# Softmax denominators of a cross attention: one f32 matmul on f32 ones becomes two f16 matmuls on f16 ones, placed after the second score group of a head

## The reference, cut to what matters

```python
q = rmsnorm(q, q_norm_w)             # 8 batches, 32 heads of 128, 64 queries
k = rmsnorm(jnp.repeat(k, 4, axis=1), k_norm_w)      # 8 key heads, 1601 keys
scores = jnp.einsum('bhqd,bhkd->bhqk', q, k) * scale + attention_mask
attn = jax.nn.softmax(scores.astype(jnp.float32), axis=-1)
out = jnp.einsum('bhqk,bhkd->bhqd', attn, v)
```

## Time and profile before

| | us |
|---|---|
| median of three runs | 2546.01 (2544.3 to 2546.27) |
| the profiled execution, its own time | 2543.32 |
| its span in the trace | 2541.5 |
| of it: up to the first full step of the attention | about 230 |
| attention, steps at full pace | about 230 to 1920 |
| attention's last step and what follows it | about 1920 to 1967 |
| output projection, state-space layer, experts | the rest |

### The profile page before, as it was taken

One profiled execution on the slowest core, in us unless ns is written; L12 is line 12 of the kernel. 1 busy time (PEld: TensorE's weight loads), 2 busy tenths in 40 slices (PEclk: granted clock), 3 DMA queues, 4 the chain that ended last, 5 costly groups with the idle time before them and its releaser, 6 DMA issues. The chain is left out here.

```text
span 2541.5 us, 48195 instructions
## 1 busy us (share of the span) xinstructions
PE 2394.1 (94%) x18380; PEld 1736.5 (68%) x18380; DVE 1996.1 (79%) x2722; ACT 1252.1 (49%) x1830; POOL 1510.8 (59%) x927
## 2 busy tenths in 40 slices
PE   6879999999999999999999999999996878989995
PEld 3447878877887787788778878877885334544543
DVE  6868787888788778888878888888777548889984
ACT  4544554455455445544544554455443435555640
POOL 0116777777777777777777777777765003344432
PEclk9989999999999999999999999999998989999997
DMA  5521000100100010001010100100000921122100
GB/s 188 175 62 28 24 23 25 32 24 19 32 25 21 27 32 24 19 25 32 18 30 26 30 17 27 32 17 16 9 6 13 286 96 59 60 93 81 59 18 25
DMA packets 101092, 117.67 MB, mean 46 GB/s; under 512 B 8190, under 2 KB 70782, under 8 KB 100862
## 3 DMA queue, kind: packets, MB, share of 16 engines
q1 hardware_dynamic: 98846, 107.25, 13.3%
q0 software_dynamic: 2016, 7.34, 1.1%
HBM read 96.74 MB, written 17.83 MB: 45 GB/s over the span
## 5 line engine op out<-in xcount | busy, mean ns | idle before, releaser
L176 POOL TENSOR_TENSOR p_l<-S,p_h 128x1792 f16<-128x1792 f32 x126 | 422.5, 3354 | 285.9 <-ACT p_h L444 285.9
L550 DVE SCALAR_TENSOR_TENSOR S<-pS,rk,mask 128x256 f32<-128x256 f32 x832 | 359.9, 478 | 137.3 <-PE pS L244 130.6
L244 PE MATMUL pF<-w_l,ctx_h 128*128 128x256 f16 (+1 forms) x1664 | 453.5, 273 | 0.0
L244 PE MATMUL pF<-w_h,ctx_l 128*128 128x256 f16 (+1 forms) x1664 | 453.5, 273 | 0.0
L244 PE MATMUL pF<-w_h,ctx_h 128*128 128x256 f16 (+1 forms) x1664 | 453.5, 273 | 0.0
L560 DVE TENSOR_REDUCE mx<-S 128x256 f32<-128x3328 f32 x64 | 382.4, 5976 | 2.2
L244 PE MATMUL pF<-ctx_h,w_h 128*128 128x400 f16 (+1 forms) x1024 | 341.1, 333 | 4.0 <-PEq L790 4.0
L244 PE MATMUL pF<-ctx_l,w_h 128*128 128x400 f16 (+1 forms) x1024 | 341.0, 333 | 0.0
L244 PE MATMUL pF<-ctx_h,w_l 128*128 128x400 f16 (+1 forms) x1024 | 340.1, 332 | 0.0
L426 ACT ACTIVATE v_h<-pF 128x512 f16<-128x512 f32 (+1 forms) x224 | 126.7, 566 | 402.6 <-PE pF L244 402.6
L650 POOL TENSOR_TENSOR sq_l<-sq_f,sq_h 128x400 f16<-128x400 f32 (+1 forms) x256 | 242.6, 948 | 63.5 <-ACT sq_h L418 63.5
(11 more groups left out here) (256 smaller groups left out, 5498.0 us busy)
## 6 DMA issues: line engine op xcount, KB each, us to landing
ctx_p<-ctxT_dram SPq DMA_DIRECT2D x42, 458.0 KB, 3.5
s_wst<-winG_dram SPq DMA_DIRECT2D x8, 1536.0 KB, 6.5
q_wst<-wqT_dram SPq DMA_DIRECT2D x8, 1024.0 KB, 7.4
o_scratch<-o_st SPq DMA_DIRECT2D x32, 256.0 KB, 2.4
p_ost<-o_scratch SPq DMA_DIRECT2D x16, 512.0 KB, 6.6
p_wst<-woT_dram SPq DMA_DIRECT2D x16, 512.0 KB, 7.6
s_wst<-winG_dram SPq DMA_DIRECT2D x8, 1024.0 KB, 5.2
m_wost<-woutG_dram SPq DMA_DIRECT2D x8, 1024.0 KB, 5.4
```

The costliest lines, as they stand in the source:

```text
L176: eng.tensor_tensor(p_l[:, s % 2, t0:t1, :], S[:, s % 2, t0:t1, :], p_h[:, s % 2, t0:t1, :], ALU.subtract).then_inc(pl_ok, 1)
L244: mm = pe.matmul(out, x, y, start=first and j == 0, stop=final and j == 2)
L550: ins = dve.scalar_tensor_tensor(out=S[:, s % 2, t, :].rearrange("p (r q) -> p r q", r=REP), in0=bank[:, t % 2, :].rearrange("p (r q) -> p ...
```

## The change

The sums are handed to TensorE as two f16 parts instead of one f32 array. `total` now makes the last add twice, once with an f16 output (`psum_hl[:, 0]`, the high part) and once in f32 (`psum_p`, now one buffer), and then subtracts the high part from the f32 sum into `psum_hl[:, 1]`, f16. A new semaphore `part_ok` counts the two parts. `denominators` makes two f16 matmuls on f16 ones that accumulate into the same place. It stands behind the second score group, and before it now stands `vals_earlier(2)`, which moves nowhere itself. Because `psum_hl` has one buffer, `total` waits for `den_ok, u` instead of `u - 1`: the denominators of the head just before must be through.

```diff
--- before.py
+++ after.py
@@ -83,12 +83,13 @@
         mx = sb("mx", [P, QC], F32)
         top = sb("top", [P, 2], F32)
         ident = sb("ident", [P, P], F32)
-        psum_p = sb("psum_p", [P, 2, QC], F32)
+        psum_p = sb("psum_p", [P, QC], F32)
+        psum_hl = sb("psum_hl", [P, 2, QC], F16)
+        ones_h = sb("ones_h", [P, P], F16)
         z = sb("z", [P, 2, 16], F32)
         rk = sb("rk", [P, 2, 16], F32)
         half = sb("half", [P, 16], F32)
         lnb = sb("lnb", [P, 1], F32)
-        ones = sb("ones", [P, P], F32)
 
         pF = [pb(f"pF{i}", [P, 512]) for i in range(3)]
         pS = [pb(f"pS{i}", [P, 2, QC]) for i in range(2)]
@@ -122,6 +123,7 @@
         pl_ok = sem("pl_ok")
         sum_ok = sem("sum_ok")
         pv_ok = sem("pv_ok")
+        part_ok = sem("part_ok")
         den_ok = sem("den_ok")
         o_ok = sem("o_ok")
         o_stored = [sem(f"o_stored{h}") for h in range(2)]
@@ -188,8 +190,13 @@
             eng.tensor_tensor(T[:, 0, :], T[:, 0, :], T[:, 1, :], ALU.add).then_inc(sum_ok, 1)
             eng.tensor_tensor(T[:, 2, :], T[:, 2, :], T[:, 12, :], ALU.add).then_inc(sum_ok, 1)
             wait(eng, sum_ok, 5 * u + 4)
-            wait(eng, den_ok, u - 1)
-            eng.tensor_tensor(psum_p[:, s % 2, :], T[:, 0, :], T[:, 2, :], ALU.add).then_inc(sum_ok, 1)
+            wait(eng, den_ok, u)
+            eng.tensor_tensor(psum_hl[:, 0, :], T[:, 0, :], T[:, 2, :], ALU.add).then_inc(part_ok, 1)
+            eng.tensor_tensor(psum_p[:, :], T[:, 0, :], T[:, 2, :], ALU.add).then_inc(sum_ok, 1)
+
+            wait(eng, sum_ok, 5 * (u + 1))
+            wait(eng, part_ok, 2 * u + 1)
+            eng.tensor_tensor(psum_hl[:, 1, :], psum_p[:, :], psum_hl[:, 0, :], ALU.subtract).then_inc(part_ok, 1)
 
         @block.sync
         def _(sp):
@@ -330,8 +337,9 @@
 
             def denominators(b, s):
 
-                wait(pe, sum_ok, 5 * (U * b + s + 1))
-                pe.matmul(pO[s % 2][:, 1, :], ones[:, :], psum_p[:, s % 2, :], start=True, stop=True).then_inc(den_ok, 1)
+                wait(pe, part_ok, 2 * (U * b + s + 1))
+                pe.matmul(pO[s % 2][:, 1, :], ones_h[:, :], psum_hl[:, 0, :], start=True, stop=False)
+                pe.matmul(pO[s % 2][:, 1, :], ones_h[:, :], psum_hl[:, 1, :], start=False, stop=True).then_inc(den_ok, 1)
 
             for i in range(NCH):
                 key_fill(i, i, 0, 0, 0, i)
@@ -366,10 +374,10 @@
                             value_fill(FILLS * eb + slot(es, NCH + i), slot(es, NCH + i), (par - (1 if s == 0 else 0) + job // (U // 2)) % 2, job, f)
 
                     scores(b, s, 0)
+                    vals_earlier(2)
+                    scores(b, s, 1)
                     if before(b, s, 2):
                         denominators(*before(b, s, 2))
-                    vals_earlier(2)
-                    scores(b, s, 1)
                     vals_earlier(3)
                     keys(0)
                     scores(b, s, 2)
@@ -508,7 +516,7 @@
             dve.memset(zr[:, :], 0.0)
             dve.memset(half[:, :], -0.5)
             dve.memset(lnb[:, :], P_LN)
-            dve.memset(ones[:, :], 1.0).then_inc(consts, 1)
+            dve.memset(ones_h[:, :], 1.0).then_inc(consts, 1)
             dve.memset(mask[:, KT - 1, :], NEG).then_inc(consts, 1)
             dve.memset(v_h[:, :, KT - 1, :], 0.0).then_inc(consts, 1)
             dve.memset(v_l[:, :, KT - 1, :], 0.0).then_inc(consts, 1)
```

## The result

| | before | after |
|---|---|---|
| median of five runs, us | 2544.3 (2541.77 to 2546.27) | 2531.23 (2528.42 to 2533.68) |
| span of the profiled execution, us | 2541.5 | 2529.4 |

The ratio after to before is 0.9948, with a 95% interval of 0.9935 to 0.9961: 13.2 us less, between 9.9 and 16.5. The prediction was 2533.6 us, 12.4 us less than the median it started from, 2546.01. That median was of three of the five runs in the table and is 1.7 us above theirs, which is most of the 2.4 us between the forecast and the result. The change made the kernel faster, by what was forecast.

The account below looks back on a forecast made before the run. TensorE was taken to bound the kernel. -13.0 us in the loop and +0.6 us in the tail made -12.4 us, from 2546.01 to 2533.6 us; own range 2531 to 2536.5, stated range 2530.5 to 2540.5.

Parts of the forecast that it names:

- What bounds the kernel: Attention's full-pace stretch: TensorE is the bound, busy 1666.57 of 1670 us, with 3.4 us of waits.
- 0.43 to 0.22 us: Denominators on TensorE, steps 3 to 64: two f16 matmuls replace one f32, 0.21 us a step, 13.0 us in all.
- The move: Denominators placed behind the second score group: TensorE's added wait costs nothing, with 3.3 us of cover remaining.
- The cover in the old place: TensorE's margin after GpSimd's sums if the denominators had not moved: about zero.
- GpSimd: One more add and a subtraction: 1.46 us a step, free in the loop; VectorE held up by less than 0.1 us.
- The cover of 2.3 us for every second step: From the end of VectorE's first evacuation to TensorE's third score group: 2.3 us; 3.6 us in steps of other parity.
- The rival that would have made it slower: Late `rk` makes TensorE wait above 3.95 us of new GpSimd work, a loss from 4.4; 2568 us; 5%.
- The port rule: VectorE's second input and GpSimd share a port; beside the new instructions VectorE reads one input from PSUM, so nothing added.
- The tail: After the last step: 0.1 through GpSimd's sums, 0.8 through VectorE's, -0.3 for matmuls; +0.6 us, bounds 0 and 1.5.
- The starting point: Forecast taken from the runs' median, 2546.01 us, 2.7 us above the profiled execution's 2543.32 us.

## Why the prediction was right, point by point

**What bounds the kernel.** Right. TensorE's 3.4 us of waits, of 1670, were the proof, and the steps follow TensorE's instructions to 0.01 us in both directions, from one to four matmuls. What I passed over is what those two waits were: I left them as a remainder, and they were the jumps of the hardware loop, 3.8 us in that execution, 4 to 9 in others, a third to two thirds of what the change itself brought.

**0.43 to 0.22 us.** Right to the hundredth: 0.21 a step read in the looped profiles, 0.217 written out. The sum, 13.0 us for 62 denominators, was measured as 13.0 for 60 and 13.4 for all 62, the last step included (25.45 to 25.24 us), on which I had 0.2 us of doubt.

**The move.** Right that it costs nothing, and that the second score group 0.43 us earlier is worth nothing to the whole. The cover in the old place, "about zero", was about zero: TensorE waited 0.05 us there in the loop, and not at all written out. So the move is worth 3 us at most with the loop, and nothing in the steps without it.

**GpSimd.** 1.46 us were predicted, 1.51 measured (0.73 for the add, 0.67 for the subtraction against my 0.65, 0.16 for the wait against my 0.08; the two adds overlap by 0.04). `rk` made VectorE 0.07 us late, within the "less than 0.1 us" that I allowed. But the 0.23 us between the end of `rk` and the evacuation, which I counted as VectorE's slack, aren't slack: in the loop the evacuation starts 0.23 us after `rk` even when VectorE has waited for it (1014.71 to 1014.94). The cover of 2.3 us for every second step showed itself at the place and at 2.0 us: I had left TensorE's third score group where it was (1013.67), but it comes 0.21 us earlier by the gain itself.

**The rival that would have made it slower** was right in its mechanism and too generous in its point: I put the first wait of TensorE at 3.95 us of new work and the change from gain to loss at 4.4. The version with four idle adds has 1.51 + 2.64 = 4.15 us of it, loses 0.67 us in such a step where the sum gives 0.2, and is as fast as the kernel before. Without the 0.23 and the 0.21 us of the paragraph above the 3.95 us become 3.5, and 4.15 - 3.5 = 0.65 is what was measured; gain turns to loss near 3.5 + 13/31 = 3.9 us.

**The port rule.** L188, which doubled to 1.47 us beside the context split, is again 1.46 to 1.48 us (as L190) in seven of eight steps and 0.73 us in the eighth and in the whole last batch, which have no such split. The two new instructions ran at 0.73 and 0.67 us in every step of both kinds. As far as this kernel shows it, the rule of the Trainium skill ("SBUF — State Buffer", Who interferes with whom) holds, and leaving it out of the sum was right.

**The tail.** +0.6 us predicted, +0.5 measured from the last maximum to the last division:

```profile
1938.24 0.73 POOL L195 TENSOR_TENSOR psum_p<-S 128x256 f32<-128x256 f32 x1
1939.05 0.67 POOL L199 TENSOR_TENSOR psum_hl<-psum_p,psum_hl 128x256 f16<-128x256 f32 x1
...
1940.42 1.76 DVE L588 RECIPROCAL o_st<-pO 128x256 f32<-128x256 f32 x1 [0.94 <-PE pO L342]
...
1949.88 0.42 DVE L194 TENSOR_TENSOR psum_hl<-S 128x256 f16<-128x256 f32 x1
...
1951.58 1.76 DVE L588 RECIPROCAL o_st<-pO 128x256 f32<-128x256 f32 x1 [0.49 <-PE pO L342]
```

The first division comes 12.02 us after the last maximum starts, instead of 11.21: 0.8 us late, where 0.85 was predicted. From there on VectorE makes both low parts without the 0.75 us wait for `p_h` that stood there, so none of it is left. From the last add's place to the last division it is 1.70 us instead of 1.22: the 0.5 us. Written out, the tail was 1.0 us longer than that of the kernel before (23.65 against 22.68 us), inside the bounds of 0 and 1.5.

**The starting point** was a median 2.7 us above the profiled execution, and I couldn't tell which was the rule. The profiles give three sources of the spread: the dip of the clock ahead of the second maximum, there or not, 1.6 us; the jumps, 3.8 to 9.0 us for the two; and the stretch behind the attention, 572.9 to 580.3 us. Written out, four runs of the changed kernel lie within 1.3 us, but those of the other four written-out kernels within 2.2 to 5.1.

## What to carry to other kernels

When one engine's order is full, price a change there by the start-to-start distance of the instructions taken out and put in. Then ask for the slack of the engine that takes over the work, up to the moment at which the full engine comes back for the result (a moment that the gain itself brings forward), since three quarters of GpSimd's time was busy here and 1.5 us more a step were still free. An f32 matmul like this one, 128x128 by 128x256 on exact ones, cost four f16 matmuls and was replaced by two, since another engine had time to make the parts. And look at the few remaining waits of a full engine before anything else: here they were 3.8 to 9.0 us, for three lines, against the 13.2 of the change.

## What the runs showed that I had not expected

A jump back of the hardware loop cost 1.9 to 4.7 us each in the profiles here, although every engine has its own loop and TensorE was full on both sides. Writing out eight batches removed it. The five kernels that were written out gained 8.7 to 11.8 us between their medians (2531.23 to 2522.49 us for the changed one), which is more than their jumps, 3.8 to 9.0 us, account for; in some pairs of profiles the rest lies behind the attention, in code that is the same, and isn't explained. In the loop, GpSimd's wait before the subtraction took 0.16 us instead of 0.08, and VectorE started 0.23 us after `rk` instead of 0.04. A GpSimd add whose two inputs are the same 128x256 array took 0.61 us, 0.69 from start to start, where one with two different ones takes 0.73.
